# A factorization kernel on one core: fields parted 10 and 3, pair products multiplied in 64-column and 32-column tiles, and ScalarE fills the block-diagonal operand

## The reference

```python
x1 = einsum('bik,bjk,hij->bhk', e, e, W1) + b1        # 128 outputs h
x2 = einsum('bik,bjk,hij->bhk', x1, e, W2) + b2
z  = sum(concat([x1, x2], axis=1), axis=-1)           # 512 x 256
h  = relu(concat([z, dense_ctx]) @ W_top1 + b_top1)   # 272 -> 512
h  = relu(h @ W_top2 + b_top2)                        # -> 256
y  = h @ W_top3                                       # -> 1
```

## Time and profile before

| what | us |
|---|---|
| median of 3 runs (lowest to highest) | 169.63 (168.71 to 170.01) |
| the profiled execution, its own time | 170.0 |
| its span in the trace | 168.1 |
| PE busy / PE weight loads busy | 137.4 / 124.0 |
| DVE busy | 111.0 |
| POOL busy | 94.9 |
| ACT busy | 65.5 |

### The profile page before, as it was taken

The page is one execution under the profiler, slowest core; times in us unless marked ns, Lnnn a source line. Parts: engine busy times, 40 slices in busy tenths (PEclk is TensorE's granted clock), DMA queues, the critical chain, the costliest instruction groups (busy, mean ns, idle before and its releaser), DMA issues.

```text
span 168.1 us, 3668 instructions
## 1 busy us (share of the span) xinstructions
PE 137.4 (82%) x1414; PEld 124.0 (74%) x1414; DVE 111.0 (66%) x425; ACT 65.5 (39%) x177; POOL 94.9 (56%) x100
## 2 busy tenths in 40 slices
PE   6418999200099979898899999899999979999995
PEld 6305666100099959788898899789899969999993
DVE  7899368999999919999804599980659996000000
ACT  1122888400025870350453730155281024574042
POOL 4778777787778777777777777777760000000000
PEclk9965999955559999999999999999999999999999
DMA  6994331000000312001011331010042000022000
GB/s 129 387 289 157 120 98 23 12 12 13 12 18 8 65 27 75 16 12 16 12 16 17 64 78 25 16 16 12 16 80 59 5 0 4 0 51 65 17 0 0
DMA packets 8537, 8.56 MB, mean 51 GB/s; under 512 B 3128, under 2 KB 7650, under 8 KB 8340
## 3 DMA queue, kind: packets, MB, share of 16 engines
q1 hardware_dynamic: 2668, 4.70, 8.8%
q10 hardware_dynamic: 2908, 2.12, 5.7%
q0 software_dynamic: 2944, 1.51, 5.3%
HBM read 7.28 MB, written 1.04 MB: 50 GB/s over the span
## 4 chain that ended last, share of the span: by engine, by line
PE 60%; DVE 16%; POOL 8%; ACT 6%; DMA 4%; issue 4%; ACTq 0%; DVEq 0%; SPq 0%
PE ring L619 15%; PE z2p L655 14%; POOL emb L317 8%; PE z2p L660 7%; PE ring L625 5%; PE h2y L711 4%; PE ring L639 4%; DVE l L507 3%; DMA emb<-in_tbl,idx 3%; DVE r L499 3%; DVE emb L478 3%; PE ring L648 2%; PE h1p L702 2%; ACT v_in L791 2%; DVE ctx_x L474 2%
## 5 line engine op out<-in xcount | busy, mean ns | idle before, releaser
L317 POOL DMA_INDIRECT emb<-in_tbl,idx x92 | 94.0, 1022 | 29.4 <-issue 27.7
L619 PE MATMUL ring<-r,l 128*128 128x104 f32 x256 | 32.7, 287 | 15.2 <-DVE l L507 15.2
L619 PEld LDWEIGHTS ring<-r,l 128*128 128x128 f32 x256 | 31.9, 203 | 16.3 <-DVE l L507 15.4
L803 ACT COPY t_in<-ring 128x416 f32<-128x416 f32 x32 | 16.2, 506 | 34.2 <-PE ring L619 34.2
L655 PE MATMUL z2p<-t_in,v_in 128*128 128x128 f32 x208 | 24.4, 277 | 0.8 <-ACT v_in L791 0.8
L655 PEld LDWEIGHTS z2p<-t_in,v_in 128*128 128x128 f32 x208 | 23.6, 192 | 1.2 <-ACT v_in L791 1.0
L590 PE MATMUL ring<-w1s,w2t 128*128 128x352 f32 x52 | 17.2, 494 | 4.0 <-DVE w1s L371 4.0
L590 PEld LDWEIGHTS ring<-w1s,w2t 128*128 128x128 f32 x52 | 10.6, 206 | 10.1 <-DVE w1s L371 4.1
L507 DVE TENSOR_TENSOR l<-sg_b,l 128x192 f32<-128x192 f32 (+5 forms) x72 | 15.6, 300 | 0.0
L507 DVE TENSOR_TENSOR l<-sg_a,l 128x192 f32<-128x192 f32 (+5 forms) x72 | 15.6, 298 | 0.0
L474 DVE TENSOR_TENSOR ctx_x<-ring,mask 128x512 f32<-128x512 f32 x6 | 4.1, 691 | 17.2 <-PE ring L639 17.1
(11 more groups left out here) (129 smaller groups left out, 183.3 us busy)
## 6 DMA issues: line engine op xcount, KB each, us to landing
w2t<-in_L_rec_W SPq DMA_DIRECT2D x1, 1664.0 KB, 7.2
emb<-in_tbl,idx POOLq DMA_INDIRECT x92, 2.4
wt<-in_W_top SPq DMA_DIRECT2D x2, 512.0 KB, 8.4
octet<-in_octet_ids SPq DMA_DIRECT2D x1, 750.0 KB
gram_scratch<-t_in ACTq DMA_DIRECT2D x4, 169.0 KB
gram<-gram_scratch ACTq DMA_DIRECT2D x4, 126.0 KB
small_tbl<-in_tbl SPq DMA_DIRECT2D x4, 125.0 KB
w<-in_L_rec_W SPq DMA_DIRECT2D x1, 338.0 KB, 7.7
```

The source lines that it names most:

```text
L317: pool.indirect_dma_start(out=emb[:, g, f * K:(f + 1) * K], out_offset=None, in_=a[f"tbl_{f}"][:, :], in_offset=bass.IndirectOffsetOnAxis( ...
L619: last = pe.matmul(ps[:, i * 4 * NF:(i + 1) * 4 * NF], l[:, t, 0:P], R[:, t, :, :].rearrange("p q f -> p (q f)"), start=True, stop=True)
L803: act.copy(t_in[:, :, n * 4 * BLK:(n + 1) * 4 * BLK], ps[:, 0:BLK * 4 * NF].rearrange("p (x j) -> p j x", j=NF)).then_inc(t_out, 1)
```

## The change

The 13 fields of a half are parted 10 and 3 instead of 7 and 6. There are then 48 inner products of two different fields in a half (36 before) and 30 across (42 before). With the 13 squares that is 61 inner columns, and a column of ones in half a.

The singles leave the 128 inner columns of `l` and get 32 columns of their own. `R` gets two columns of ones a sample (28 instead of 26). The blocks of a group are now:

- block 0: the singles, 32 columns of `l` against 52 of `R`, 32 matmuls in four 32-column tiles of TensorE (each tile writes its own 32 partitions of the bank);
- blocks 1 to 8: inner pairs, each 4 tiles `t` with two matmuls of 64 columns (half a and half b, in two 64-column tiles) against 108 columns of `R`;
- blocks 9 and 10: across pairs, each 16 tiles `t` with four matmuls of 32 columns against 28 columns of `R` (7 of the 14 columns a sample of the other half), in four 32-column tiles.

`v_ac` and the across part of `z_group` have 7 matmuls instead of 13. The Gram part is four matmuls still: two of them read sums against the column of ones (in `t_in` and `t_ac`), and only the sums of singles of half a against half b go through DRAM. These DMAs, four stores and two loads a group, move from ScalarE's queue to SyncE's, between the waits by which it passes on that a group's fields have landed.

The copies into `R` move from VectorE (4 a part) to ScalarE (`fill_r`, 4 a part, read from `l` instead of PSUM). `fill_r(g + 1)` stands in ScalarE's order behind the block copies of group g and ahead of `z_copy(g)`. Small changes go with it: the across products on VectorE are three instructions a half of 10 fields each (before 7 of 6), the layout of `vh_ac` and of the Gram weights, some memsets, no memset of `t_ac`, and the look-ups stand behind blocks 5 and 7 of the eleven (before 4 and 6 of twelve).

```diff
@@ -27,25 +27,30 @@
...
-Q1 = (NH + 1) // 2
+Q1 = 10
...
-SGL = NIN
-ONE = SGL + NH
+ONE = NIN
...
-MC = ACR + NX
...
+ACW = 32
...
+L_AC, L_SG = P, P + 2 * ACW
+LW = L_SG + ACW
+ONES = (0, NH + 1)
+RF = NF + 2
+NS = 7
+TF = NF + 1
...
-XBLK = 8
-TB = NB + NT // XBLK
-LW = 2 * (HALF + NX)
+XBLK = 16
+GBLK = NT // 4
+TB = 1 + NB + NT // XBLK
...
-OH_AT = (4, 6)
+OH_AT = (5, 7)
...
@@ -53,11 +58,11 @@
...
@@ -267,14 +271,33 @@
...
         def lc(c, col, n):
...
+            o = c * HALF + col if col < HALF else L_AC + c * ACW + col - HALF
...
+        def single(c, f, n):
...
+            return l[:, :, L_SG + c * NH + f:L_SG + c * NH + f + n]
...
+        def rcol(f):
...
+            return 1 + f if f < NH else 2 + f
...
+        def tcol(f):
...
+            return f if f < NH else f + 1
...
         def vcol(c, js, col, n):
...
+            return vh_in[:, js, c * HALF + col:c * HALF + col + n]
...
+        def vac(c, late):
...
+            o = c * HALF + (0 if late else ACW)
+            return vh_ac[:, 0 if late else 1:NS, o:o + NX]
...
+        def of_late(late):
...
+            return slice(NS - 1, NH) if late else slice(0, NS - 1)
...
@@ -296,6 +319,18 @@
...
+                sp.wait_ge(t_out, TB * g + 1)
+                if g > 0:
+                    sp.wait_ge(gram_in, 32 * g)
+                    sp.wait_ge(z1_done, g)
+                by_pair = gram_dram.rearrange("(u v) b -> u v b", v=NH)
+                for q in range(4):
+                    s = slice(q * P // 4, (q + 1) * P // 4)
+                    sp.dma_start(by_pair[:, :, s], t_sg[q * P // 4:q * P // 4 + NH, :, :]).then_inc(gram_stored, 16)
+                sp.wait_ge(gram_stored, 64 * (g + 1))
+                for i in range(2):
+                    o = GOFF[2 + i] - GOFF[2]
+                    sp.dma_start(gram[0:GCH[2 + i], i, :], gram_dram[o:o + GCH[2 + i], :]).then_inc(gram_in, 16)
...
@@ -491,31 +538,31 @@
...
-                dve.tensor_copy(lc(c, SGL + o, w), sgt[c][:, :, o:o + w]).then_inc(singles_out, 1)
-                if g > 0 and part == 0:
-                    dve.wait_ge(t_done, TB * g)
-                for q in range(4):
-                    s = slice(K * q, K * (q + 1))
-                    last = dve.tensor_copy(R[s, :, q, f0:f1], sgt[c][s, :, o:o + w])
-                last.then_inc(r_ready, 1)
+                dve.tensor_copy(single(c, o, w), sgt[c][:, :, o:o + w]).then_inc(singles_out, 1)
...
+                return dve.tensor_tensor(lc(c, 0, NH), sgt[c], single(c, 0, NH), ALU.mult)
...
             def products(c, runs):
...
-                                             lc(c, SGL + p, 1).to_broadcast([P, NT, n]), ALU.mult)
+                                             single(c, p, 1).to_broadcast([P, NT, n]), ALU.mult)
...
-            across = [(ACR + p * Q2, p, Q1, Q2) for p in range(Q1)]
...
+            def across(c):
+                for i in range(Q2):
+                    last = dve.tensor_tensor(lc(c, ACR, NX).rearrange("p t (x q) -> p t x q", q=Q2)[:, :, :, i], sgt[c][:, :, 0:Q1],
+                                             single(c, Q1 + i, 1).to_broadcast([P, NT, Q1]), ALU.mult)
+                return last
...
             def build_a(g):
...
-                products(0, inner + across).then_inc(pairs, 2)
+                products(0, inner)
+                across(0).then_inc(pairs, 2)
...
             def build_b(g):
...
@@ -523,7 +570,7 @@
...
+                across(1).then_inc(pairs, 1)
...
             def split_wt1c():
...
@@ -607,23 +657,36 @@
             def t_block(g, n, first):
...
+                    pe.wait_ge(r_ready, 3 * (g + 1))
+                elif n == 1:
...
+                elif n == 1 + NB:
...
+                if bank_free("t", TB * g + n):
+                    pe.wait_ge(*bank_free("t", TB * g + n))
...
+                if n == 0:
+                    w = 4 * NH
+                    for i in range(GBLK):
+                        for q in range(4):
+                            t = q * GBLK + i
+                            last = pe.matmul(ps[q * ACW:(q + 1) * ACW, i * w:(i + 1) * w], l[:, t, L_SG:LW],
+                                             R[:, t, :, rcol(NH):RF], start=True, stop=True)
+                elif n <= NB:
+                    w = 4 * TF
...
+                        t = (n - 1) * BLK + i
+                        for c in range(2):
+                            last = pe.matmul(ps[c * HALF:(c + 1) * HALF, i * w:(i + 1) * w], l[:, t, c * HALF:(c + 1) * HALF],
+                                             R[:, t, :, 1:RF], start=True, stop=True)
...
+                    w = 4 * NS
...
+                        t = (n - 1 - NB) * XBLK + i
+                        for q in range(4):
+                            o = L_AC + q // 2 * ACW
+                            last = pe.matmul(ps[q * ACW:(q + 1) * ACW, i * w:(i + 1) * w], l[:, t, o:o + ACW],
+                                             R[:, t, :, (3 - q) * NS:(4 - q) * NS], start=True, stop=True)
...
             def look_up(g, ks=(0, 1)):
...
@@ -641,23 +704,26 @@
...
             def gram_part(g):
...
+                pe.wait_ge(gram_in, 32 * (g + 1))
...
+                z1p = bank_of("z1", g)[:, 0:P]
+                pe.matmul(z1p, wg[:, 0, :], t_in[:, NH, :], start=True, stop=False)
+                pe.matmul(z1p, wg[:, 1, :], t_ac[:, 0, :], start=False, stop=False)
+                for i in range(2):
+                    w = GCH[2 + i]
+                    last = pe.matmul(z1p, wg[0:w, 2 + i, :], gram[0:w, i, :], start=False, stop=(i == 1))
...
             def z_group(g, first, tail=False):
...
                 def inner(j0, j1, start=False, stop=False):
...
+                        last = pe.matmul(zp[1], v_in[:, j, :], t_in[:, tcol(j), :], start=(start and j == j0), stop=(stop and j == j1 - 1))
...
                 def across(start=False, stop=False):
...
+                    for j in range(NS):
+                        last = pe.matmul(zp[1], v_ac[:, j, :], t_ac[:, j, :], start=(start and j == 0), stop=(stop and j == NS - 1))
...
@@ -674,7 +740,7 @@
...
+                pe.wait_ge(t_out, TB * g + 1 + NB)
...
@@ -799,33 +864,31 @@
             def copy_block(g, n):
...
+                if n == 0:
+                    if g > 0:
+                        act.wait_ge(gram_stored, 64 * g)
+                    act.copy(t_sg[:, :, :], ps[:, 0:GBLK * 4 * NH].rearrange("p (x j) -> p j x", j=NH)).then_inc(t_out, 1)
+                elif n <= NB:
+                    act.copy(t_in[:, :, (n - 1) * 4 * BLK:n * 4 * BLK],
+                             ps[:, 0:BLK * 4 * TF].rearrange("p (x j) -> p j x", j=TF)).then_inc(t_out, 1)
...
+                    m = n - 1 - NB
+                    act.copy(t_ac[:, :, m * 4 * XBLK:(m + 1) * 4 * XBLK],
+                             ps[:, 0:XBLK * 4 * NS].rearrange("p (x j) -> p j x", j=NS)).then_inc(t_out, 1)
...
+            def fill_r(g):
+                for part, (f0, f1) in enumerate(PARTS):
+                    act.wait_ge(singles_out, 3 * g + part + 1)
+                    if part == 0:
+                        if g == 0:
+                            act.wait_ge(zeroed, 2)
+                        else:
+                            act.wait_ge(t_done, TB * g)
+                    c = f0 // NH
+                    for q in range(4):
+                        s = slice(K * q, K * (q + 1))
+                        last = act.copy(R[s, :, q, rcol(f0):rcol(f0) + f1 - f0], single(c, f0 - c * NH, f1 - f0)[s])
+                    last.then_inc(r_ready, 1)
...
             def z_copy(g, order):
...
@@ -849,15 +912,12 @@
...
+            fill_r(0)
...
+            for n in range(EARLY, len(pre)):
...
+            fill_r(1)
...
             def group(g):
...
@@ -865,14 +925,12 @@
...
+                fill_r(g + 1)
...
```

More of the change, by code:

```diff
@@ L192, in build @@
         t_out = sem("t_out")
[L193 to L194 removed]
+        gram_stored = sem("gram_stored")
         gram_in = sem("gram_in")
@@ L225, in build @@
         EARLY = len(pre)
-        pre += [("v_ac", j, n) for j, n in cut(NH, 4)]
+        pre += [("v_ac", j, n) for j, n in cut(NS, 4)]
         LATE = len(pre)
@@ L403, in mixed_terms @@
                     sums(vcol(c, js, col, n).rearrange("p j (x q) -> p x q j", x=1), p, 1, q, n)
-                for p in range(Q1):
-                    last = sums(vcol(c, slice(0, NH), ACR + p * Q2, Q2).rearrange("p j (x q) -> p x q j", x=1), p, 1, Q1, Q2)
+                for late in (True, False):
+                    jl = of_late(late)
+                    first = m(0, Q1, Q1, Q2)[:, :, :, jl]
+                    second = m(Q1, Q2, 0, Q1).rearrange("p q x j -> p x q j")[:, :, :, jl]
+                    for x0, x1 in ((0, Q1 // 2), (Q1 // 2, Q1)):
+                        last = dve.tensor_tensor(vac(c, late).rearrange("p j (x q) -> p x q j", q=Q2)[:, x0:x1],
+                                                 first[:, x0:x1], second[:, x0:x1], ALU.add)
                 last.then_inc(vh_mixed, 1)
@@ L417, in add_unmixed @@
```

(21 more changed lines are left out.)

104 lines of the change are left out of this document (30 added, 74 removed).

## The result

The changed kernel takes 174.29 us (median of 4 runs, 174.1 to 176.38) beside 169.45 of the kernel before (4 runs). The ratio is 1.032, 95% interval 1.024 to 1.039: slower, where 162.1 was forecast. The profiled execution took 176.38 us, with a span of 174.6; it is the longest of the runs, so its trace shows about 2 us more than the median has.

What follows compares the result with a forecast made beforehand. VectorE was taken to bound the kernel up to 45.8 us, TensorE behind it. 168.1 - 5.7 (layer 1 of group 2) - 0.4 (blocks) - 1.35 (z_group) = 160.6 span, 162.1 us as median; range 159.5 to 170.5.

Steps and rivals of the forecast that it cites:

- how fast fours can start: Four-tile across blocks: four matmuls with their loads every 45 ns, 2.9 us a group, no change.
- The closing sentence: Fails if four tiles don't run side by side, turns between tilings cost several times 0.1 us, or PE runs out of instructions.
- ScalarE's hold: `z_copy` and layer 1 stand behind the next group's `fill_r`: 1.2 us given back in group 0.
- The clock: Group 0's blocks: starting near 42.8 us, the half clock passes under less of the work; blocks end at 55.5, not 58.2.
- 64-column tiles: Inner blocks: two tiles with 108 columns take 93 ns a pair instead of 111, -1.2 us a group.
- z_group's 7 matmuls and the Gram part: z_group: across matmuls fall from 13 to 7, -1.35 us a group on the path; Gram part keeps four.
- Group 0: Its blocks start sooner, block 1 at 44.8 us instead of 45.86; v_in transposes come 5.9 us sooner, -4.7 left after `z_copy`.
- The gathers as a limit: Gather landings hold `fill_r`: layer 1 at 101.8 us in group 1, 129.7 at the earliest in group 2, limiting the gain.
- starts that limit a four to 90 ns: Rival on four-tile blocks: across 5.8 and singles 1.4 us a group add 3.6; 173.1 us, chance 0.16.
- The 60 cycles a matmul of the Trainium skill: Overhead per matmul; if it held for the whole engine, 100 ns a four, ending a little above 173.1 us.

Runs made afterwards that it cites:

- e2: The changed kernel with the first across block put behind the third inner block instead of the eighth, same instructions; 168.10 and 167.73 us.
- e3: The changed kernel with half of the across matmuls, each 56 columns wide instead of 28; 161.20 us, ratio 0.945 to the kernel before.
- e10: The kernel before with each across matmul issued three times over; 195.63 us, ratio 1.149.
- e1: The changed kernel with `fill_r` split: part 0 ahead of `z_copy`, part 1 behind it, part 2 between the next group's relus; 167.26 us, ratio 0.989 to before.
- e8: The changed kernel with the copies into `R` back on VectorE and `fill_r` gone; 167.71 us, ratio 0.986 to the kernel before.
- e5: The changed kernel with the edits of e1 and e2 together; 165.08 us, ratio 0.971 to the kernel before.
- e4: The kernel before with each inner 128-column matmul made two of 64 columns in two tiles; 166.28 us, ratio 0.979.
- e7: The kernel before with 64-column inner matmuls and, in group 0 alone, the copies into `R` on ScalarE; 164.32 us, ratio 0.967.

## Why the prediction was wrong

**The step that failed is the one on how fast fours can start.** I weighed 28 to 90 ns a four from the array and from the starting of records, and took 45. The array does it in 35 in a burst, under my value. But the across blocks took 5.0 to 5.5 us a group, 78 to 86 ns a four, where the sum has 2.9: 9.2 us more in all; the time was missed by 12.2. What I did not price is where the instructions come from: 970 more records, each with its load, are seven more lots of 256. The closing sentence named it among the things that would make the prediction fail, without a price, and the row that has it (q8, 11 packets) stood on the page. A price could have been had: the across pairs take 4 instructions in 45 ns, 11.3 each, but only 256 in a row; over a longer stretch the trace before showed nothing that fast. 512 in a row were outside what it bore out, and I read a rate of one lot as a rate without end. e2, e3 and e10 show it from three sides. What sets the 3.5 us from lot to lot no run shows.

**ScalarE's hold was right in kind, too small, and in groups 1 and 2 had the wrong cause.** I put `fill_r` at 4.2 us in group 0; it took 5.43, with copies of 32x416 at 560 ns, just over my upper bound of 5.3. I gave back 1.2 us for it. PE waited 2.73, 2.2 more than in e1, and the half clock behind that, which I left out, added 0.8 in layer 1 (3.20 us from its start to relu, 2.42 before) and 1.6 in layer 2. e1 has the hold away for 7.0 us in all, e8 for 6.6; some of that is gaps that fell differently, and in e5 against e2, with fewer gaps, it is worth about 3.

For group 1 I let `fill_r(2)` wait for the last part's landing at 99.8 and counted 0.6 us of VectorE's work behind it; of VectorE I said that in groups 1 to 3 nothing is on the path. The trace has VectorE on it: half b's singles come 5.5 us behind the end of the blocks, because half a's products stand ahead of them, and VectorE waits for no landing there. From the end of the blocks to layer 1 are 9.9 us in group 1 and 10.0 in group 2. In e3, with z_group at the full clock, PE waits 1.7 us ahead of layer 1 in both groups where e5 has 0.46: about as much as z_group's shorter across part had saved there. I did not follow VectorE's order through, though the description of the kernel has it start only when the blocks have ended.

**The clock.** I counted it in group 0's blocks only. The kernel after loses it again behind its own waits. In e3, without gaps, z_group of group 3 runs at the full clock. But e8 has a gap of 2.4 us in the same place and keeps its clock there. It is the same with ScalarE's hold: e2 has a wait of 2.73 us ahead of layer 1 too and runs layer 2 in 2.15 us, at the full clock. So a gap makes the loss possible and not certain; what decides stays open.

**64-column tiles**: 93 ns a pair was the step. The row "42.41 7.91" begins at the lower clock; in group 3 the 56 pairs in a row take 5.33 us, 95 ns each, and e4 has 92 for 104 columns. Right. e4 gained 3.4 us, inside its 3 to 4.5.

**z_group's 7 matmuls and the Gram part**: the 14 across records take 1.56 us where 26 took 2.90. Right in size; in groups 1 and 2 the hold took it back.

**Group 0**: block 1 was forecast at 44.8 and came at 42.4, since the last gathers were issued 2 us sooner in this run; e8, with the copies back on VectorE, starts it at 43.8. Of the 3.4 us, then, ScalarE's copies themselves gave about 1.4, as they did in e7 against e4 (44.24 for 45.71). The other 2.0 were there in e8 before any copy into `R`: VectorE takes the first part of group 0 at 23.79, in the kernel before at 25.91. Why the gathers of group 0 came sooner no run shows.

**The gathers as a limit**: behind group 0 they never came to bind, as PE was late itself. In e5, where both losses are smaller, layer 1 of group 1 starts at 100.67 and of group 2 at 130.11. The prediction has 101.8 and 129.7 for them, and 160.6 for the span, which is 162.2 there with 2.0 us of issue waits left. That is near, and in part by luck: what sets 130.11 is PE's own work, with across blocks of 17.2 us where 11.6 were forecast, and not the landing from which 129.7 was worked out.

**The rivals**: starts that limit a four to 90 ns were given 0.16 and 173.1 us. The time is near that, as a four took 78 to 86 ns on the average of a stretch, and the mechanism is not: inside a burst starts take 8.7 ns. It would have been right by luck. The 60 cycles a matmul of the Trainium skill (TensorEngine Tiling, Instruction Overhead) don't hold across column tiles in this trace, by the same figure. An effect on the supply would have been its own rival.

## What to carry to other kernels

A matmul in small tiles saves array time and costs instructions: when a change multiplies them, count them against a supply, over a stretch longer than one lot, and not against the array alone. Work that moves to an idle engine stands in that engine's order; what stands behind it there has to be asked first, and splitting it around the urgent step was worth 3 to 7 us here (e5 against e2, e1 against the changed kernel). The same holds for the engine that feeds it: a step that waits for VectorE's last piece waits for all that stands ahead of that piece. Parts of a change should be tried apart: two of this one's gain 6 us together (e7, 170.32 to 164.32 on its chip), the others took them back and more.

## What the runs showed of the hardware

- PE's instructions came in packets of 16 KB, 256 instructions. In group 3 a burst of exactly 128 records, with 3.46 us to the start of the next (3.46 in e1 too, 3.73 in e8), shows the supply at its limit, some 13.5 ns an instruction (3.46 us by 256). The q8 packets there lie 3.4 to 3.5 us apart.
- Four 32-column tiles with 28 moving columns in float32 ran at 35 ns a four inside a burst, with 56 columns at 61 ns (e3, with no gap).
- Two 64-column tiles took 92 ns a pair with 104 columns, against 111 for one 128-column matmul.
- A ScalarE copy of 32x416 from SBUF to SBUF took 560 ns, beside 506 for 128x416 from PSUM; a quarter of the partitions was no cheaper.
- PE's granted clock fell to its lower level about 1.4 us after a wait of 2.73 us had ended, during dense work, and stayed there through layer 2. Behind the same wait it fell in e3 too and was back for layer 2 (2.16 us), and in e2 it did not fall.
